# Four edits in one kernel: the ends of the first attention, attention masks as products, when the state-space terms are computed, and the first and last capacity expert

## The reference

```python
x = x + xattn0(ctx, ln(x), mask)     # a: 8 heads of 64; keys, values from context AND latents
x = x + attn0(ln(x))                 # b: causal, 2-D: 8 sequences of 64, 16 heads of 32
x = x + ffn0(ln(x))                  # c: shared expert + 8 routed, top 2
x = x + xattn1(ln(x), ctx)           # d: top-32 cross attention, FiLM, S4D state space, MLP
x = x + attn1(ln(x))                 # e: causal, rotary, one k/v head
x = x + ffn1(ln(x))                  # f: 8 experts, each takes its 160 best tokens
# a: q = rms(ln(lat) @ Wq.T), k = rms([ln(ctx) @ Wk.T, ln(lat) @ Wlk.T]); softmax over 1601 + 64 keys
# b, e: logits = where(triu(1), -inf, q @ k.T) * scale; softmax; @ v
# f: per expert: vals, idx = top_k(gate, 160); y.at[idx].add(vals * (relu(x[idx] @ W1) @ W2))
```

## Time and profile before

| | us |
|---|---|
| median of 3 runs (2566.6, 2568.47, 2572.2) | 2568.47 |
| the profiled execution | 2571.8 |
| its span, first to last instruction | 2570.1 |
| PE busy / PEld / DVE / ACT / POOL | 2252.9 / 1355.7 / 1046.6 / 735.0 / 407.7 |
| stage a | 0 to 932 |
| stage b | 933 to 1042 |
| stage c | 1043 to 1493 |
| stage d | 1493 to 2097 |
| stage e | 2098 to 2199 |
| stage f | 2200 to 2563 |
| stage z | 2565 to 2570 |

### The profile page before, as it was taken

How to read it: one execution, slowest core, us unless ns; L and a number is a source line. 1 busy time by engine, 2 the same in 40 slices (tenths; PEclk the granted TensorE clock), 3 DMA queues, 4 the chain that set the end, 5 groups by cost and what they waited for, 6 DMA issues and landing times. The chain is left out here.

```text
span 2570.1 us, 26983 instructions
## 1 busy us (share of the span) xinstructions
PE 2252.9 (88%) x10194; PEld 1355.7 (53%) x10194; DVE 1046.6 (41%) x2139; ACT 735.0 (29%) x1462; POOL 407.7 (16%) x469
## 2 busy tenths in 40 slices
PE   5799999999999886789999987896998966599996
PEld 2355555555555443444444445555464434499996
DVE  4245646645655114210000059888393035422110
ACT  2234544544544211111111133434262101111111
POOL 0000000000000000289997111212000000000001
PEclk8899999999999987899999996776898987799998
DMA  5001221221221320578888562431400010556652
GB/s 194 26 13 48 67 72 50 69 72 47 72 76 48 108 74 17 196 294 310 317 319 306 182 241 77 154 115 53 177 16 17 0 67 2 220 212 245 227 202 92
DMA packets 131538, 327.33 MB, mean 127 GB/s; under 512 B 39857, under 2 KB 89169, under 8 KB 111826
## 3 DMA queue, kind: packets, MB, share of 16 engines
q1 hardware_dynamic: 99392, 297.20, 32.2%
q10 hardware_dynamic: 29202, 19.49, 2.4%
q0 software_dynamic: 2816, 8.92, 1.1%
HBM read 303.22 MB, written 21.24 MB: 126 GB/s over the span
## 5 line engine op out<-in xcount | busy, mean ns | idle before, releaser
L868 PE MATMUL a_mix<-a_xn,a_probs_T 128*128 128x384 f32 (+1 forms) x832 | 313.2, 493 | 13.9 <-issue 9.7
L797 PE MATMUL a_sc<-a_wk_centred,a_ctx_T 128*128 128x512 f32 x624 | 289.7, 601 | 4.3 <-DVE a_keys L462 2.3
L1774 PE MATMUL c_gate_up<-c_w_wide,c_h_rows 128*128 128x512 f32 x480 | 210.9, 592 | 0.0
L868 PEld LDWEIGHTS a_mix<-a_xn,a_probs_T 128*128 128x128 f32 (+1 forms) x832 | 145.6, 191 | 119.2 <-issue 71.7
L797 PEld LDWEIGHTS a_sc<-a_wk_centred,a_ctx_T 128*128 128x128 f32 x624 | 118.4, 193 | 130.7 <-issue 106.7
L1679 DVE TENSOR_TENSOR c_hidden<-c_silu,c_gate_up 128x512 f32<-128x512 f32 x38 | 26.1, 687 | 354.5 <-PE c_gate_up L1774 342.1
L1774 PEld LDWEIGHTS c_gate_up<-c_w_wide,c_h_rows 128*128 128x128 f32 x480 | 90.1, 190 | 108.1 <-issue 108.1
L462 DVE SCALAR_TENSOR_TENSOR a_keys<-a_k_bias,a_std,a_sc 128x512 f32<-128x512 f32 (+1 forms) x104 | 77.1, 741 | 171.4 <-PE a_sc L797 171.4
L2198 PE MATMUL f_ring<-f_picked_T,f_w 128*128 128x160 f32 x1024 | 145.3, 302 | 1.0 <-DVE f_picked_T L2039 1.0
L2198 PEld LDWEIGHTS f_ring<-f_picked_T,f_w 128*128 128x128 f32 x1024 | 141.7, 192 | 1.3 <-DVE f_picked_T L2039 1.1
L2213 PE MATMUL f_ring<-f_hidden,f_w 128*128 128x160 f32 x1024 | 141.2, 300 | 0.4 <-ACT f_hidden L2100 0.4
(11 more groups left out here) (496 smaller groups left out, 3508.5 us busy)
## 6 DMA issues: line engine op xcount, KB each, us to landing
c_w_wide<-in_L_ffn_W SPq DMA_DIRECT2D x68, 1024.0 KB, 7.1
f_w<-in_L_ffn_W SPq DMA_DIRECT2D x32, 2048.0 KB, 8.6
c_w_down<-in_L_ffn_W SPq DMA_DIRECT2D x34, 1024.0 KB, 7.4
a_ctx_T<-in_ctx_T SPq DMA_DIRECT2D x48, 384.0 KB, 3.6
a_xn<-in_ctx SPq DMA_DIRECT2D x24, 768.0 KB, 7.2
d_context_T<-in_ctx_T SPq DMA_DIRECT2D x24, 768.0 KB, 11.1
d_context<-in_ctx SPq DMA_DIRECT2D x8, 2304.0 KB
mixed_context<-a_mixed_T ACTq DMA_DIRECT2D x84, 64.0 KB, 1.8
```

The costliest lines, as they stand in the source:

```text
L797: last = pe.matmul(key_bank(b, t), ctx_T[:, n % AHEAD, k, cols], wk_centred[:, k, :], start=(k == 0), stop=(k == KC - 1))
L868: ins = pe.matmul(mix[:, 0:DC], probs_T[0:m, t, p * P:(p + 1) * P], xn[0:m, b % 2, t, :], start=(t == 0), stop=(t == CT - 1))
L1774: last = pe.matmul(gate_up[2 * (u % 2) + part][:], h[:, k, :], w_wide[:, i % WIDE_RING, k, :], start=(k == 0), stop=(k == KD - 1))
```

## The change

Four parts, all in one kernel.

**First attention.** At the start the second layer norm stands behind the scaling of Wk, and two small loads stand ahead of Wk's on ACT's queue. In sequence 0 `scale_heads` runs at t - 3 ahead of `sum_heads`, which runs at t - 2; `root_heads` at t - 3, `turn_heads` at t - 4, `put_queries` at t - 5; the first two `latent_values` stand at t = 12 in the loop and not behind it. At the end `output_heads` and `output_tokens` stand one pair further back.

**Masks.** `pick_row` (a one-hot matrix) times `mask_row` (0 or -1e30), both bf16, is put into the score bank by 16 products of 64 x 512 for each pair of tiles, and the score products add to it. DVE's mask adds go; the maximum and the difference read PSUM. `scores`, `top` and `total` have one buffer for each tile. In stage b the values' products and DVE's `put_values` are spread among the scores.

**State space.** Its DVE and ACT parts stand at u = 3; `make_shares` stays at u = 1.

**Experts.** Expert 0's rows come from `pick` by a product (`pick_rows`), with no token list and gather. The last expert's rows are added by a product from PSUM (`turn_pick`, `put_rows`, DVE `summed`), with no store and gather; both gathers of the others wait for one expert fewer. Each quarter of x is stored as it is finished; stage z is gone.

The diff, cut to what the text speaks of:

```diff
@@ stage a, vector
             norm.on_vector(dve, g.x, g.hn)
-            norm.on_vector(dve, g.hn, g.hn, 1)
...
                 dve.tensor_scalar(wk[:, k, :], wk[:, k, :], gain[:, k:k + 1], None, ALU.mult).then_inc(wk_scaled, 1)
+            norm.on_vector(dve, g.hn, g.hn, 1)
             dve.wait_ge(means_full, 1)
...
                     if b == 0 and 0 <= t - 3 < 2 * NT:
-                        sum_heads(t - 3)
-                    if b == 0 and 0 <= t - 4 < 2 * NT:
-                        scale_heads(t - 4)
+                        scale_heads(t - 3)
+                    if b == 0 and 0 <= t - 2 < 2 * NT:
+                        sum_heads(t - 2)
@@ stage a, tensor, the last pairs
-            for p in range(PAIRS):
...
-                turn_mix(n)
...
-                output_heads(p)
...
-                output_tokens(p)
+            last_mix(1, 0, 3)
+            turn_mix(last)
+            last_mix(1, 3, CT)
+            for p in range(2, PAIRS):
+                last_mix(p, 0, 3)
+                turn_mix(last + p - 1)
+                last_mix(p, 3, 7)
+                output_heads(p - 2)
+                last_mix(p, 7, CT)
+                output_tokens(p - 2)
+            output_heads(PAIRS - 2)
+            turn_mix(last + PAIRS - 1)
+            output_tokens(PAIRS - 2)
+            output_heads(PAIRS - 1)
+            output_tokens(PAIRS - 1)
@@ stages b and e
             def centre(t):
-                if t >= 2:
-
-                    dve.wait_ge(ring_full, R_TILE + 4 * (t - 2) + 2)
 
                 dve.wait_ge(scores_full, t // 2 + 1)
-                for i in range(4):
-                    dve.tensor_tensor(scores[:, t % 2, 4 * i:4 * i + 4, :], bank[i][:, t % 2, :, :],
-                                      causal[:].unsqueeze(1).to_broadcast([P, 4, SEQ]), ALU.add).then_inc(masked, 1)
...
+                mine = bank[:, :, t % 2, :, :]
...
+            act.wait_ge(mask_made, 2)
+            for i in range(4):
+                r = slice(HD * i, HD * i + HD)
+                act.activation(pick_row[r], picked[r, i], ACT.Copy).then_inc(rows_made, 1)
+                act.activation(mask_row[r], hidden[r, i], ACT.Copy).then_inc(rows_made, 1)
...
             def pair_scores(pair):
                 if pair >= 1:
-                    pe.wait_ge(masked, 8 * pair)
+                    pe.wait_ge(centred, 2 * pair)
+                for h in range(2):
+                    for b in range(2):
+                        for i in range(4):
+                            r = slice(HD * i, HD * i + HD)
+                            pe.matmul(bank[b * SEQ:b * SEQ + SEQ, i].rearrange("p t c k -> p (t c) k"),
+                                      pick_row[r, h, :], mask_row[r, h, :].unsqueeze(1).to_broadcast([HD, 8, SEQ]),
+                                      start=(h == 0), stop=False, skip_group_check=True)
@@ stage b, tensor
+                ready()
+                pair_scores(0)
+                values(0)
+                values(1)
+                pair_scores(1)
+                values(2)
+                values(3)
@@ stage b, vector
+                centre(0)
+                centre(1)
+                divide(0)
+                put_values(0)
+                divide(1)
+                put_values(1)
+                centre(2)
+                put_values(2)
+                centre(3)
+                put_values(3)
+                divide(2)
+                divide(3)
@@ stage c
                 if u == 1:
+                    make_shares()
+                if u == 3:
                     ss.on_vector(dve)
-                    make_shares()
...
-                if u == 1:
+                if u == 3:
                     ss.waves_on_scalar(act)
@@ stage f
+            def pick_rows():
+                pe.wait_ge(rows_out, E_N)
+                pe.wait_ge(picks_ready, NT)
+                for k in range(KD):
+                    j, at = divmod(k * CAP, 3 * CAP)
+                    for t in range(NT):
+                        last = pe.matmul(turned[j][:, at:at + CAP], g.hn[:, t, k * P:(k + 1) * P], pick[:, 0, t, :],
+                                         start=(t == 0), stop=(t == NT - 1))
+                last.then_inc(picked_full, 1)
...
+            pick_rows()
             list_tokens(0)
-            turn_rows(0)
...
+            def put_rows():
+                pe.wait_ge(pick_T_out, 2)
+                pe.wait_ge(tokens_ready, E_N)
+                for j, (lo, hi) in enumerate(PARTS):
+                    pe.wait_ge(y_out, 2 * LAST + j + 1)
+                    for t in range(NT):
+                        last = pe.matmul(put[t][:], pick_T[0:hi - lo, j, t * P:(t + 1) * P], y[0:hi - lo, LAST % 2, j, :],
+                                         start=(j == 0), stop=(j == 1))
...
+            for t in range(NT):
+                sp.wait_ge(summed, t + 1)
+                sp.dma_start(tokens(g.out)[:, t, :], g.x[:, t, :]).then_inc(stored, 16)
```

More of the change, by code:

```diff
@@ L770, in _ @@
                                ).then_inc(o_out, 1)
+            last = PAIRS * (NB - 1)
+            put_back(last)
+            put_mix(last + 1)
+            for p in range(2, PAIRS):
+                put_back(last + p - 1)
+                put_output_heads(p - 2)
+                put_mix(last + p)
+            put_output_heads(PAIRS - 2)
+            put_back(last + PAIRS - 1)
+            put_output_heads(PAIRS - 1)
         @block.tensor
@@ L1186, in _, with put_values @@
                     dve.sem_inc(ring_out, 1)
-            for t in range(NT):
+            def put_values(t):
                 u = R_V + t
@@ L1224, in divide @@
                                   ALU.mult).then_inc(probs_ready, 1)
-            centre(0)
-            for t in range(NT):
-                if t + 1 < NT:
-                    centre(t + 1)
-                divide(t)
+            if rope:
+                for t in range(NT):
+                    put_values(t)
+                centre(0)
+                for t in range(NT):
+                    if t + 1 < NT:
+                        centre(t + 1)
+                    divide(t)
+            else:
+                centre(0)
+                centre(1)
[9 more added lines that the diff above has]
+                divide(3)
@@ L1285, in _, with values @@
                 last.then_inc(ring_full, 1)
-            for t in range(NT):
+            def values(t):
                 u = R_V + t
@@ L1946, in _ @@
                         load_w2(n)
+            for t in range(NT):
+                sp.wait_ge(summed, t + 1)
+                sp.dma_start(tokens(g.out)[:, t, :], g.x[:, t, :]).then_inc(stored, 16)
+            sp.wait_ge(stored, 16 * NT)
         @block.gpsimd
@@ L1956, in _ @@
             pool.wait_ge(hn_stored, 16)
-            for e in range(E_N):
+            for e in range(1, E_N):
                 pool.wait_ge(tokens_ready, e + 1)
-                if e >= 2:
+                if e >= 3:
                     pool.wait_ge(picked_full, e - 1)
@@ L2076, in _ @@
                     dve.tensor_tensor(g.x[:, t, :], back[:, t, :], g.x[:, t, :], ALU.add).then_inc(added, 1)
+            dve.wait_ge(added, 2 * NT)
+            for t in range(NT):
+                dve.wait_ge(put_full, t + 1)
+                dve.tensor_tensor(g.x[:, t, :], put[t][:], g.x[:, t, :], ALU.add).then_inc(summed, 1)
         @block.scalar
@@ L2133, in _ @@
                     put_hidden(e, n)
-                for j in range(len(DOWN)):
-                    put_y_T(e, j)
-            put_y(E_N - 1)
+                put_y_T(e, 0)
+                if e == LAST:
+                    act.wait_ge(pick_turned, 1)
+                    for j, (lo, hi) in enumerate(PARTS):
+                        act.activation(pick_T[0:hi - lo, j, :], turned[j][0:hi - lo, :], ACT.Copy).then_inc(pick_T_out, 1)
+                put_y_T(e, 1)
+            put_y(LAST)
         @block.tensor
@@ L2243, in _ @@
                     down(e, j)
-            turn_y(E_N - 1)
+                    if e == LAST and j == 0:
+                        turn_pick()
+            turn_y(LAST)
+            put_rows()
 S4 = 64
```

191 lines of the change are left out of this document (101 added, 90 removed).

## The result

The changed kernel takes 2479.91 us (median of 4 runs, 2478.13 to 2480.52) against 2567.53 for the kernel before (median of 4, 2565.63 to 2572.20). The ratio is 0.9655, 95% interval 0.9638 to 0.9672. The forecast was 2476 with a range of 2464 to 2496. Executions of one kernel differ: the kernel before mostly ran near 2566 or near 2574, its medians beside the later experiments were 2568.64, 2575.17, 2573.55 and 2572.34, so ratios taken beside different ones of these do not compare to better than 0.3%, and one execution of e8, at 11215 us, is left out of its median.

The account below looks back on a forecast made before the run. PE was busy 2252.9 of 2570.1 us, so waits and half-clock PE time bounded the gain. Eight terms summed to 92.0: 2571.8 gave 2479.8, less 3.3 for the median, 2476 us, range 2464 to 2496.

Parts of the forecast that it names:

- Start of a, 5.4: First attention's start: scaled Wk comes earlier with the second norm behind it and beside L890; 5.4 us saved.
- Sequence 0, 29.8: First attention's heads' products: 20.0 us of waits for DVE go, and 9.8 of half clock with them.
- Rivals 1 and 2: 1: clock stays down where waits go, 18 us lost, chance 0.10; 2: new ring in sequence 0, 20 lost, 0.10.
- End of a, 10.2: First attention's end: 13.4 us of waits and half clock around output_heads, less 3.2 kept; 10.2 saved.
- Masks in e, 8.7: Later masked attention: DVE's mask adds and a wait go, 16 mask products a pair come at 0.9; 8.7 us saved.
- Rival 3: Masks: their products don't run side by side; 9.7 us lost in e, 6.4 in b, time 2492, chance 0.05.
- Reading PSUM: DVE's maximum and difference cost the same from PSUM as from on-chip memory; by the skill's rule, 1 us less saved.
- Masks in b, 10.1: Earlier masked attention: DVE's chain follows the masks, then the copy of v is late; 10.1 us saved.
- State space, 10.0: Stage c: PE's wait of 8.51 us for unit 2's c_hidden goes, with 1.5 of clock; 10.0 saved.
- rival 5: Late weights in stage c (first half) and waits that stay in f (second); 10 us lost, time 2486, chance 0.08.
- Start of f, 11.3: Capacity experts: expert 0's wide begins earlier, pick_rows taking 4.4 us; 11.3 saved, 5 with half clock and slow first records.
- Rival 4: Whole kernel: PE without pauses is granted less clock over dense stretches; 2575 us or more, chance 0.02.

Follow-up runs that it names:

- e8: The changed kernel plus 17 products of ident by ident, read by nobody, in PE's wait ahead of pick_rows; 2478.25 us, ratio 0.9631.
- e5: The kernel before with the new order of sequence 0's loop alone; 2540.44 us, ratio 0.9873.
- e6: The changed kernel with stage b's values' products all ahead of the scores again, as before; 2481.55 us, ratio 0.9641.
- e3: The kernel before with the state-space part at unit 3 alone; 2563.10 us, ratio 0.9955.
- e1: The kernel before with the first attention's part alone (start, sequence 0, end); 2523.58 us, ratio 0.9799.
- e7: The changed kernel with v copied tile by tile and, from expert 1 on, the next token list one piece of wide earlier; 2472.26 us, ratio 0.9602.
- e12: The changed kernel with tile-wise copy of v, earlier token lists and 17 unread products ahead of pick_rows, exponentials left in place; 2471.28 us, ratio 0.9613.

## Why the prediction was right, and where its terms were not

**Start of a, 5.4.** Measured 5.1 in the combined kernel (5.85 from DVE's start on), 5.9 alone. The step that the norm lies beside L890 held, with one turn: L890 ran in 4.5, so the norm came last in its place, as the text had said it would.

**Sequence 0, 29.8.** Right in mechanism and size: the last probabilities are turned 35.3 earlier in the combined kernel (817.05 against 852.32), start and loop together, against 35.2. That it agrees to 0.1 is luck: the same point lies between 848.4 and 856.0 in five profiles without these parts and between 815.6 and 820.1 in seven with both. The term that looked least sure, 9.8 for the clock, was paid in e5: 592 ns a record and no waits. Rivals 1 and 2 are out.

**End of a, 10.2.** 11.0 combined and 12.6 alone. I had kept 3.2 of waits; 1.1 of ACT's was left. `turn_mix` of the last pair (0.5) now stands between `output_heads(2)` and `output_tokens(2)` and covers most of that copy, which I had not counted.

**Masks in e, 8.7.** 9.6, by terms that partly cancel. The mask products were mis-sized: 0.46 for 16 at full clock, 0.86 at half, where I took 0.9. Pair 0's cost nothing at all: DVE's first maximum comes 50.0 into the stage, where the first mask add came 50.1 in, because PE had waited 0.34 at that place. Pair 1's made DVE wait 0.49, where I took 0.2. A wait of DVE for ACT's last exponential, 0.78, was in no term. And the last tile's turning follows DVE's last division by 0.6, where it had followed by 1.4, which was in no term either. Rival 3 is out.

**Reading PSUM.** The equal prices held: 1.22 from PSUM (stage b above) and 1.22 from on-chip memory. The Trainium skill's fixed difference between the two (VectorE: DVE Perf Modes, section on the TRN2 errata) doesn't show in these records of 1024 elements, nor in the distance between their starts (1.26 and 1.14 here, 1.25 and 1.14 in the kernel before).

**Masks in b, 10.1.** About 11 by the change, 10 of it by the masks and 1 by the order of the values (e6). The chain was the forecast one (masks, DVE's chain of 18.1, then the copy of v), with the copy 1 longer and the tiles 1 shorter. The other 3 of the measured 14.3 were the clock of the execution that stood for before, at L1283 and L1347. The step that failed is that I took one execution's length of a stage as the stage's length.

**State space, 10.0.** 10.8 and 10.1 (e3). The weights are no later (PE waits 3.2 for them, before 3.4): rival 5's first half is out.

**Start of f, 11.3.** Measured 9.5. The mis-sized step is `pick_rows` at 0.138 a record: I had taken full clock although PE stands still for 4.0 just ahead of it (3.60 in the row of before). e8 shows that this is the cause. I had it as a bound, not as the value.

**End of f, 6.5.** 6.2.

**The rest of f.** 3.5 for rows that came late to experts 1 to 7 was in no term. It is the second half of rival 5 on a small scale. I had put what the masks do to stage f at nothing without a reason, and every profile with them has 4.8 to 5.6 of these waits, against 1.3 to 3.6 without. That this gather has no slack could be read from the profile of before, since three of the later experts waited in it already.

**Rival 4** (less clock from denser work): the mean granted clock rose from 0.917 to 0.935.

**The sum.** Stage b above and stage f below forecast cancelled, by luck. Without the 3.1 of clock in b the profiles show 89.6 saved, 2.4 under the forecast: f is 5.9 short, and a, b, c and e give about 1 each more. The forecast of the median had taken off another 3.3, because the profiled execution of before lay that much over its median; the one of the changed kernel lies 0.4 below its own (2479.49 against 2479.91). So the time of the profiled execution was forecast to 0.3 and the median to 3.9. The 3.3 may be the same 3.1 of clock in b; no run shows that.

## What to carry to other kernels

A wait of 3 us in a loop cost half as much again, because the products behind it ran at half clock: count both when a wait goes, and when one stays ahead of short work. Before a stage's length of one profile is taken for a sum of small terms, look at the same stage in other profiles of unchanged code: here it moved by 4 to 8 us in places with pauses. An experiment's profile needs the same care: the 4.8 of e6 looked like the worth of an order, and 3.7 of it was the clock. A difference that is there in every profile with an edit and in none without it is hardly chance, even in a stage whose code the edit doesn't touch. When a copy through DMA becomes what is late, issue it piece by piece as its source is finished; that gave more here than the order of the engines around it.

## What the runs showed of the hardware

- Sixteen bf16 products of 32 rows by 64 columns with 512 moving columns took 0.46 us at full clock and 0.86 at half, 29 ns each, while one record of 512 f32 columns takes 0.43: some fifteen times the work side by side. That is more than the eight tiles I had counted on at the f32 price; whether bf16 or the packing gives the other factor of two no run here parts.
- The same code behind the same waits runs at either clock for its first microseconds, by execution: 27.7, 29.4 or 29.9 us for 64 records and 14.0, 15.4 or 15.6 for 32 (e3, before, e1), and 14.0 or 16.3 for the same 32 in e7 and e12.
- Seventeen products of no use in a pause of 4 us made the 32 records behind it 1.7 faster.
- Where PE waited for a gather of 160 rows by indirect DMA in the changed kernel, it had them 7.3 to 8.1 us after POOL's first issue; in the kernel before, where it did not wait, it took the rows 6.9 to 7.1 us after it.
- One copy of v of 1 MB within on-chip memory was there 7.1 us after v was complete; issued in four parts as v was made, it was not waited for (e7).
